# Edge lists and part of x on a second DMA queue, and VectorE's edge arithmetic ahead of the first norm

## What is computed

```python
edge_index = jnp.stack([src, dst])
h = jnp.maximum(_layernorm(x, axis=-1), 0.0)
x = x + _L0_gnn_ref(h, edge_attr_32, src, dst, L0_gnn_W, L0_gnn_b, L0_gnn_eps)
h = jnp.maximum(_layernorm(x, axis=-1), 0.0)
x = x + _L1_gnn_ref(h, L1_gnn_weight, L1_gnn_w_comp, L1_gnn_self_loop_weight, ..., src, dst, edge_type_86)
h = jnp.maximum(_layernorm(x, axis=-1), 0.0)
x = x + _L2_gnn_ref(h, edge_index, edge_weight, L2_gnn_W, L2_gnn_b)
h = jnp.maximum(_layernorm(x, axis=-1), 0.0)
x = x + _L3_gnn_ref(h, src, dst, L3_gnn_W, L3_gnn_b)
```

## Time and profile before

| | us |
|---|---|
| median of three runs | 8661.93 |
| the profiled execution | 8675.0 |
| its span (first to last instruction) | 8673.2 |
| busy POOL / PE / DVE / ACT in it | 6224.3 / 4674.7 / 4395.6 / 2234.2 |
| first gather of layer 0 starts at | 56.59 |

### The profile page before, as it was taken

The page is one execution under the profiler, slowest core; times in us unless marked ns, Lnnn a source line. Parts: engine busy times, 40 slices in busy tenths (PEclk is TensorE's granted clock), DMA queues, the critical chain, the costliest instruction groups (busy, mean ns, idle before and its releaser), DMA issues. The chain is left out here.

```text
span 8673.2 us, 104883 instructions
## 1 busy us (share of the span) xinstructions
PE 4674.7 (54%) x23835; PEld 4127.8 (48%) x23836; DVE 4395.6 (51%) x8833; ACT 2234.2 (26%) x5812; POOL 6224.3 (72%) x6577
## 2 busy tenths in 40 slices
PE   4555555555777777777774444444445444444444
PEld 3444444444677777777773333333333333333333
DVE  6555555555688888888884222222223222222222
ACT  1000000002688788888881000000000000000000
POOL 6777777776666666666665777777775777777776
PEclk6555555556555555555555555555555555555555
DMA  4111111113788888888881000000000000000001
GB/s 84 26 26 26 26 26 26 26 26 97 232 245 245 244 246 243 246 244 246 245 243 34 13 13 13 13 13 13 13 13 18 13 13 13 13 13 13 13 13 18
DMA packets 599594, 726.39 MB, mean 84 GB/s; under 512 B 339548, under 2 KB 433308, under 8 KB 596385
## 3 DMA queue, kind: packets, MB, share of 16 engines
q0 software_dynamic: 290064, 544.60, 24.1%
q1 hardware_dynamic: 309497, 181.39, 7.6%
HBM read 685.53 MB, written 40.64 MB: 84 GB/s over the span
## 5 line engine op out<-in xcount | busy, mean ns | idle before, releaser
L511 POOL DMA_INDIRECT lanes<-table,idx x4764 | 4522.7, 949 | 1546.7 <-issue 1451.4
L1277 PE MATMUL ps<-arena 128*128 128x128 f32 x9528 | 2718.5, 458 | 3232.5 <-DVE arena L1005 2337.4
L1277 PEld LDWEIGHTS ps<-arena 128*128 128x128 f32 x9528 | 2267.9, 328 | 3644.8 <-issue 3570.0
L511 POOL DMA_INDIRECT arena<-table,idx x1664 | 1581.3, 950 | 756.7 <-issue 485.1
L1005 DVE TENSOR_TENSOR arena<-lanes,ps 128x512 f32<-128x512 f32 x794 | 545.7, 687 | 2858.5 <-DMA lanes<-table,idx 2858.5
L586 ACT COPY idx<-tabs 128x4 int32 (+1 forms) x1191 | 228.3, 193 | 5727.9 <-DMA lanes<-table,idx 5723.1
L992 DVE TENSOR_TENSOR arena<-ps,node 128x512 f32<-128x512 f32 (+1 forms) x1588 | 1048.3, 680 | 0.0
L1269 PE MATMUL ps<-lanes 128*128 128x32 f32 x3328 | 752.2, 402 | 485.1 <-issue 281.4
L1269 PEld LDWEIGHTS ps<-lanes 128*128 128x128 f32 x3328 | 725.4, 330 | 511.8 <-issue 511.8
L1377 PE MATMUL ps<-t,arena 128*128 x3328 | 955.0, 402 | 0.0
L1377 PEld LDWEIGHTS ps<-t,arena 128*128 128x128 f32 x3328 | 860.3, 318 | 0.1
(11 more groups left out here) (201 smaller groups left out, 2908.9 us busy)
## 6 DMA issues: line engine op xcount, KB each, us to landing
arena<-step_rows SPq DMA_DIRECT2D x416, 256.0 KB, 4.6
lanes<-table,idx POOLq DMA_INDIRECT x4764, 2.4
arena<-table,idx POOLq DMA_INDIRECT x1664, 4.1
table<-arena SPq DMA_DIRECT2D x24, 1088.0 KB, 6.0
lanes<-in_edge_attr SPq DMA_DIRECT2D x384, 64.0 KB
table<-h SPq DMA_DIRECT2D x18, 256.0 KB, 2.4
edge_rows<-arena SPq DMA_DIRECT2D x1, 2496.0 KB, 8.4
lanes<-self_loop_table,selfi POOLq DMA_INDIRECT x98, 2.4
```

The source lines that it names most:

```text
L511: pool.indirect_dma_start(out=into, out_offset=None, in_=tableD[l], in_offset=bass.IndirectOffsetOnAxis(ap=index, axis=0)).then_inc(there, 16)
L1277: last = mm(ps[:, bass.ds(w[u], WB * D)], onehotw[:, k, u, :], wmsg[:, k, u].rearrange("p w f -> p (w f)"), start=False, stop=True, skip_g ...
```

## The change

A second DMA queue, ScalarE's, is used. SP keeps x blocks 0 to 63 (X_SP = 64), then loads types, weights and the attribute tail. ScalarE issues src, dst and the shifted dst, then x blocks 64 to 96 and the last 84 nodes under a semaphore of their own (`x_end_loaded`), and does so ahead of all its other work; it then casts the destinations, and only after that come the squares and the root of `norm(0)` and the casts of the types. VectorE does the integer arithmetic on the edges and the comparisons first (waiting for `ends_loaded`) and `norm(0)` after them, waiting for SP's part of x at its first piece and for ScalarE's part at its fifth. SP writes the source rows ahead of table 0, and TensorE transposes the source rows ahead of the count.

```diff
@@ block.sync
-            sp.dma_start(x[:, 0:nb, :], x_in[0:nb * P, :].rearrange("(b p) f -> p b f", p=P)).then_inc(x_loaded, 16)
+            sp.dma_start(x[:, 0:X_SP, :], x_in[0:X_SP * P, :].rearrange("(b p) f -> p b f", p=P)).then_inc(x_loaded, 16)
             sp.wait_ge(pads_set, 4)
-            sp.dma_start(x[0:LAST_NODES, nb, :], x_in[nb * P:N_NODES, :]).then_inc(x_loaded, 16)
...
-            edge_rows(raw[:, 0], dst, 0, ends_loaded)
-            edge_rows(raw[:, 1], dst, 1, ends_loaded)
-            edge_rows(raw[:, 2], src, 0, ends_loaded)
-            edge_rows(raw[:, 3], etype, 0, kinds_loaded)
-            edge_rows(rows[:, :, RWGT, :], weight, 0, kinds_loaded)
+            edge_rows(sp, raw[:, 3], etype, 0, kinds_loaded)
+            edge_rows(sp, rows[:, :, RWGT, :], weight, 0, kinds_loaded)
...
             sp.dma_start(by_tile[:, :, DST:, :], rows[:, :, DST:, :]).then_inc(rows_out, 16)
-            put_table(0)
             sp.wait_ge(rows_ready, 1)
             sp.dma_start(by_tile[:, :, RSRC, :], rows[:, :, RSRC, :]).then_inc(rows_out, 16)
+            put_table(0)
@@ block.scalar
-            norm(0, 0)
+            act.wait_ge(pads_set, 4)
+            edge_rows(act, raw[:, 2], src, 0, ends_loaded)
+            edge_rows(act, raw[:, 0], dst, 0, ends_loaded)
+            edge_rows(act, raw[:, 1], dst, 1, ends_loaded)
+            nb = BLOCKS - 1
+            act.dma_start(x[:, X_SP:nb, :], x_in[X_SP * P:nb * P, :].rearrange("(b p) f -> p b f", p=P)
+                          ).then_inc(x_end_loaded, 16)
+            act.dma_start(x[0:LAST_NODES, nb, :], x_in[nb * P:N_NODES, :]).then_inc(x_end_loaded, 16)
             act.wait_ge(ends_loaded, 9 * 16)
             nc.scalar.copy(rows[:, :, DST, :], raw[:, 0]).then_inc(rows_cast, 1)
+            norm(0, 0)
             act.wait_ge(kinds_loaded, 6 * 16)
@@ block.vector
-            dve.wait_ge(x_loaded, 32)
-            norm(0, lambda b: nc.vector.memset(msg[:, 1, 0, b:b + 1], 0.0))
-            dve.wait_ge(rows_cast, 1)
-            for c in range(ROWCH):
-                last = ts(before[:, c, :], thr[:, :], rows[:, c, DST, P - 1:P], None, ALU.is_gt)
-            last.then_inc(before_ready, 1)
             dve.wait_ge(ends_loaded, 9 * 16)
...
+            dve.wait_ge(rows_cast, 1)
+            for c in range(ROWCH):
+                last = ts(before[:, c, :], thr[:, :], rows[:, c, DST, P - 1:P], None, ALU.is_gt)
+            last.then_inc(before_ready, 1)
+            def piece_of_x(b):
+                if b == 0:
+                    dve.wait_ge(x_loaded, 16)
+                if b == X_SP // BLOCKS_IN:
+                    dve.wait_ge(x_end_loaded, 32)
+                return nc.vector.memset(msg[:, 1, 0, b:b + 1], 0.0)
+            norm(0, piece_of_x)
@@ block.tensor: the transposes of the source rows (wait rows_ready, src_T) now stand ahead of the count (wait before_ready, count_done)
```

More of the change, by code:

```diff
@@ L240, in gnn @@
         x_loaded = sem("x_loaded")
+        x_end_loaded = sem("x_end_loaded")
         loaded = sem("weights_loaded")
@@ L320, in gnn, with edge_rows @@
         stored = sem("output_stored")
+        X_SP = 4 * BLOCKS_IN
+        def edge_rows(engine, to, of, shift, there):
+            n_full = FULL_CH * P * P
+            n_tail = n_full + TAIL_TILES * P
+            engine.dma_start(to[:, 0:FULL_CH, :], of[shift:n_full + shift].rearrange("(c p e) -> p c e", p=P, e=P)
+                             ).then_inc(there, 16)
+            engine.dma_start(to[0:TAIL_TILES, FULL_CH, :],
+                             of[n_full + shift:n_tail + shift].rearrange("(p e) -> p e", e=P)
+                             ).then_inc(there, 16)
+            engine.dma_start(to[TAIL_TILES:TAIL_TILES + 1, FULL_CH, 0:HALF - shift],
+                             of[n_tail + shift:N_EDGES].rearrange("(a e) -> a e", a=1)).then_inc(there, 16)
         block = ctx.enter_context(nc.Block())
@@ L326, in _ @@
         def _(sp):
-            n_full = FULL_CH * P * P
-            n_tail = n_full + TAIL_TILES * P
-            nb = BLOCKS - 1
-            sp.dma_start(x[:, 0:nb, :], x_in[0:nb * P, :].rearrange("(b p) f -> p b f", p=P)).then_inc(x_loaded, 16)
+            sp.dma_start(x[:, 0:X_SP, :], x_in[0:X_SP * P, :].rearrange("(b p) f -> p b f", p=P)).then_inc(x_loaded, 16)
             sp.wait_ge(pads_set, 4)
-            sp.dma_start(x[0:LAST_NODES, nb, :], x_in[nb * P:N_NODES, :]).then_inc(x_loaded, 16)
[L334 to L342, removed]
-            edge_rows(raw[:, 0], dst, 0, ends_loaded)
-            edge_rows(raw[:, 1], dst, 1, ends_loaded)
-            edge_rows(raw[:, 2], src, 0, ends_loaded)
-            edge_rows(raw[:, 3], etype, 0, kinds_loaded)
-            edge_rows(rows[:, :, RWGT, :], weight, 0, kinds_loaded)
+            edge_rows(sp, raw[:, 3], etype, 0, kinds_loaded)
+            edge_rows(sp, rows[:, :, RWGT, :], weight, 0, kinds_loaded)
             sp.dma_start(attrD[0:N_EDGES - MAIN * ROUND * P, :], edge_attr[MAIN * ROUND * P:N_EDGES, :]
@@ L1208, in _ @@
             pe.wait_ge(ident_ready, 2)
+            pe.wait_ge(rows_ready, 1)
+            for c in range(ROWCH):
+                n = P if c < FULL_CH else TILES - FULL_CH * P
+                last = nc.tensor.transpose(ps[:, c * P:c * P + n], rows[0:n, c, RSRC, :], ident[0:n, 0:n])
+            last.then_inc(src_T, 1)
             pe.wait_ge(before_ready, 1)
@@ L1214, in _ @@
             last.then_inc(count_done, 1)
[L1216 to L1220, removed]
             pe.wait_ge(extra_ready, 1)
```

## The result

The changed kernel took 8681.65 us, the median of 22 runs (8671.51 to 8697.6), the kernel before 8668.39 us in its 22 runs; one of these, of 8905.6 us, was a slow one and is left out of the ratio. The ratio is 1.0016, with a 95% interval of 1.001 to 1.0022: 13.9 us slower, between 9 and 19. Both programs on another chip gave 1.0013 (1.0004 to 1.0022). The forecast was +9.4 us and "the same within 0.2%": the sign is right, the difference is under 0.2%, and the size is 4.5 us short, though the interval reaches down to it. The limit of 0.2% was wide: the interval of the measurement is 0.06% to either side, so that a loss of 0.16% is told from none. As a time the forecast was 8671.3 us, 10.4 us under what was measured; 6.5 us of that is the kernel before, 8661.93 us in its first three runs and 8668.39 us in all 22.

The account below looks back on a forecast made before the run. Layer 0's unbroken GpSimd gather queue was taken as the bound, so only the first gather's shift counts. List landing at 22.4 less 13.0 gave +9.4 us on 8661.9: 8671.3 us (+0.11%, "same"), range 8660 to 8683.

Parts of the forecast that it names:

- one unbroken queue of gathers: GpSimd in layer 0: 1587 steps of 1.26 us, 2003.4 us, so the first gather's shift is the kernel's whole shift.
- The pieces of VectorE's chain: VectorE before the first gather: norm 20.5, comparisons 2.5, edge arithmetic 7.9, L884 to L910 7.7, L916 and L917 2.0; sum 40.6 us.
- E: Time when the source and destination lists have landed and VectorE can start; taken as 22.4 us, alternatives 17.8 and 28.5.
- L369 (now L367) at E + 26.8: Write held by ScalarE's type cast behind the norm's root: norm starts at E + 10.4, root 14.8 us in, cast 1.58.
- L485 at E + 38.2: GpSimd's read of edge_rows, after the first write's 8.4 us and the source rows' 3.0 (2.3 to 4.4); range E + 37.5 to 39.6.
- 5.4 us to the first gather: GpSimd from L485's start: L485, two L491 and the issue times, putting the first gather at E + 43.6.
- Table 0: Its 1.6 MB write, queued behind both row writes, costs 4.3 us more at 376 GB/s: E + 42.5.
- E - 13.0: Shift of the first gather: E less 14.84 us, when x landed before, plus 1.85 us that the new order costs.
- The cover of ScalarE's cast: ScalarE's cast of the destinations, queued behind its x loads, stays hidden from VectorE by 2 us at least.
- Rival 2: Second queue's DMAs start only after SP's 1.05 MB of x: E = 26.8, +13.8 us, 8676 us; chance 0.08.
- Rival 1: Queues add up, lists move at their own 211 to 282 GB/s: E 12.6 to 15.5, -0.4 to +2.5, 8663 us; chance 0.22.
- Rival 3: Slower by over 0.2%: lists land last of all loads, E = 32.5, +19.5 us, 8681 us; decides from E = 30.3; chance 0.08.

Follow-up runs that it names:

- both tries: The changed kernel, and the kernel before with one 1.9 us comparison done 32 times more on VectorE ahead of the edge arithmetic; the latter took 8718.37 us, ratio 1.0065.
- the types first: The changed kernel with ScalarE's two casts of the types ahead of the squares and root of the first norm; one time, 8686.37 us.

## Why the prediction was right, and where it was off

- The bound, one unbroken queue of gathers: right. 2003.3 us from the first to the last in the changed kernel, no new wait. That a shift of the first gather is a shift of the time fits both tries: 12.13 us gave 13.9 (9 to 19), 61.6 gave 56.5 (43 to 70).
- The pieces of VectorE's chain: right to 0.1 us. `extra_ready` was forecast at E + 31.8 and L902 ends at 56.95, 31.9 behind 25.01; the indices at E + 40.6, measured 65.68, 40.7.
- L369 (now L367) at E + 26.8: measured 51.80, E + 26.8. L485 at E + 38.2, range to 39.6: measured E + 39.1. The source rows, queued behind the first write, cost near the upper end of their range.
- From there 5.4 us to the first gather: measured 4.6. The two reads of attributes took 1.08 and 0.91 us instead of 1.65 and 1.42. One error is +0.9 us, the other -0.8, and it is luck that they cancel: E + 43.7 where E + 43.6 was forecast.
- Table 0, forecast at E + 42.5 and so 1.1 us inside: the first gather shows no wait for it (0.31 us idle, "issue"). When it landed isn't in the views.
- **E is the term that was mis-sized**: 25.0 instead of 22.4. The bytes were right (5.07 MB moved by 24.0 us, forecast 5.15 by the landing), and so was the equal service of the two queues. The rate was wrong: I took 282 GB/s, that of SP's queue at 24 to 28 us, on the ground that two queues fill the gaps of one. They filled little: 220 to 230 GB/s until 18 us and 234 until 22; over 2 to 24 us it was 230 where one queue had moved 206 before, and from the 2.6 us of the forecast on 237, not 282. By the formula of the prediction, E - 13.0, the measured E gives +12.0 us; the first gather moved by 12.13, and the time by 13.9 (9 to 19).
- The cover of ScalarE's cast was forecast as 2 us at least and was 0.7: the cast ended at 32.26 us, VectorE came to it at 32.96. I had left out a table load of 1.28 us, and ScalarE's issue of the last piece of x took 13.35 us. SP's long issue, which I had moved to ScalarE, stayed as well: its second DMA took 7.60 us to issue.
- Rival 2, the second queue's issues coming late: right in small part. By 4 us ScalarE's queue had moved 0.01 MB against SP's 0.28, by 8 us 0.49 against 0.79; by 14 us it was ahead, 1.49 against 1.06. The start did move less (146 GB/s from 2 to 4 us, 189 before), but that is 0.09 MB, some 0.4 us at 230 GB/s. In number this rival came as close as the forecast: E = 25.0 lies between the 22.4 of the forecast and its 26.8, and the 13.9 us that were measured are its 13.8, with 9.4 just inside the interval. It is the mechanism that speaks against it: it had SP's x moved first and then 282 GB/s, whereas the queues were served side by side from 4 us on, at less.
- Rival 1, queues that add up, was wrong and had 0.22; all that speaks for it is the 230 against 206 GB/s. Rival 3 needed an E behind 30.3.

## What to carry to other kernels

The loads shared one rate of transfer whichever engine issued them, so what makes a tile arrive earlier is fewer bytes issued ahead of and beside it: one wait that held back the other queue brought the lists forward by 10.8 us, the second queue alone made x 5.8 us later. Moving a step ahead on a saturated engine gains only if its inputs are there before the old first step could start; compare landing times before reordering. And after a reorder look for the cheap producer that was moved behind the long stage (here a cast of 1.6 us behind a norm of 20), though removing it gives only what the next chain leaves.

## What the runs showed of the hardware

**The clock of TensorE in the short stages between layers, and behind the last, differs from run to run.** The profiled spans differ by 5.7 us though the last gather came 13.9 us later (8645.92 against 8632.00 us), since what follows it, mostly the last product, took 8.2 us less. The windows of that product, first before, then after (the granted clock is the third column from the end):

```profile
8650.00:8660.00 10.00, 10.00 (x31) 6.33 (x30) 1.66 (x3) 1.77 (x4) 0.00 (x0) 0.50 0.33 52
8660.00:8670.00 10.00, 9.96 (x28) 5.70 (x26) 1.76 (x4) 0.85 (x2) 0.00 (x0) 0.50 0.34 54
```
```profile
8654.00:8664.00 10.00, 10.00 (x31) 6.33 (x30) 0.76 (x2) 3.13 (x6) 0.00 (x0) 0.50 0.16 26
8664.00:8668.00 4.00, 4.00 (x20) 2.45 (x18) 1.32 (x2) 1.55 (x3) 0.00 (x0) 0.87 0.41 66
8668.00:8675.00 7.00, 7.00 (x39) 4.46 (x37) 1.90 (x3) 1.07 (x4) 0.00 (x0) 1.00 0.69 109
```

TensorE had been busy for 41% of the time at the lower level (0.50 of 2.4 GHz) through layer 3, in both runs, then ran without a gap; in the changed kernel's run the granted clock rose (0.87 in the mean of 8664 to 8668 us, then 1.00) while this product still ran, in the other it stayed at 0.50 to the end. The eight profiled runs, without the two on the chip where the kernel before took 10398 us, line up by the mean granted clock of a stretch. From the last gather to the end: 41.2 to 41.3 us at 0.50 (four runs), 38.2 at 0.54, 33.0 and 33.1 at 0.66 and 0.65, 30.6 at 0.72. From layer 0's last gather to the next one: 55.6 and 55.7 us at 0.50, 52.6 at 0.53, 49.8 and 47.6 at 0.60 and 0.61, 45.1 to 45.4 at 0.65. The changed kernel is in both lists twice, with 33.0 and 41.3 us, and 47.6 and 45.1. What makes the clock rise in one run and not in the next isn't shown. The four such stretches add up to 172.8 us in one run and 197.1 in another, more than the change moved.

**The pace of the gathers differs from run to run too.** Layers 2 and 3, where all these programs are alike, took 1980.8 to 1981.1 us each from first to last gather in four of the eight runs and 1983.3 to 1984.8 in the other four; the changed kernel is in both groups. The spread of single runs of one program is 8646 to 8682 us in one series. These two differences have that size; that they explain all of it wasn't tried.

**GpSimd's indirect DMAs take longer beside VectorE's long operations.** The two reads of attributes took 1.65 and 1.42 us in the kernel before, with VectorE's L916 and L917 running; 1.08 and 0.91 in the changed kernel, with short operations only; 1.94 and 1.75 with the types first, beside the steps of 1.9 us. The read of `edge_rows` took 1.09 us beside short operations and 1.73 beside L925 and L926. By the Trainium skill, SBUF — State Buffer, section "Who interferes with whom", VectorE and GpSimd share a port pair, which VectorE in a two-port mode, or GpSimd, holds for a whole instruction if it comes first; `tensor_tensor` has no such mode and, with both inputs in SBUF, contends with GpSimd's reads, and a probe did not see it stall a DMA. The rows agree in kind for the casts and `tensor_scalar`; the 1.94 us ran beside two `tensor_tensor` of fp32 alone, so there they differ from that probe. No run here took the port alone.
